# Two-layer cross-attention block, 128 sequences on one core: queries, keys and maxima turned on VectorE and moved by DMA in place of TensorE transposes

## The reference

```python
h = ln(x);  q, k, v = h@wq * 0.25, h@wk, h@wv;  q, k = rope(q), rope(k)
x = x + softmax(causal(q @ k.T)) @ v @ wo            # self-attention, "s"
h = ln(x);  q = rope(h@wq2 * 0.25);  k = rope(ctx@wk2);  v = ctx@wv2
x = x + softmax(q @ k.T) @ v @ wo2                   # cross-attention, "c"
x = x + gelu(ln(x)@fc1 + b1) @ fc2 + b2
a = softmax(x @ ctx.T) @ ctx
out = x + tanh(concat(x, a) @ trans_W + trans_b)
```

## Time and profile before

| | |
|---|---|
| median of 3 runs | 3412.29 us (3411.74 to 3413.0) |
| the profiled execution, its own time | 3413.38 us |
| its span in the profile | 3411.6 us |
| busy: PE, DVE, ACT, POOL | 3271.9, 2442.0, 2218.7, 1447.0 us |
| mean granted clock of TensorE | 0.983 of full speed |

### The profile page before, as it was taken

The page is one execution under the profiler, slowest core; times in us unless marked ns, Lnnn a source line. Parts: engine busy times, 40 slices in busy tenths (PEclk is TensorE's granted clock), DMA queues, the critical chain, the costliest instruction groups (busy, mean ns, idle before and its releaser), DMA issues.

```text
span 3411.6 us, 98793 instructions
## 1 busy us (share of the span) xinstructions
PE 3271.9 (96%) x40908; PEld 2779.5 (81%) x40908; DVE 2442.0 (72%) x5068; ACT 2218.7 (65%) x4737; POOL 1447.0 (42%) x2180
## 2 busy tenths in 40 slices
PE   3799999999999999999999999999999999999997
PEld 2588888888888888888888888888888888888886
DVE  3577777777777777777777777777777777777773
ACT  0366667667666666666676676666666666766764
POOL 0344444444444444444444444444444444444431
PEclk7799999999999999999999999999999999999998
DMA  3000000000000000000000000000000000000000
GB/s 88 20 16 20 27 20 20 27 20 20 27 20 22 25 20 27 21 20 27 20 20 27 20 20 27 20 22 25 20 26 21 20 27 20 20 27 20 20 13 10
DMA packets 83132, 79.62 MB, mean 23 GB/s; under 512 B 11904, under 2 KB 82432, under 8 KB 82688
## 3 DMA queue, kind: packets, MB, share of 16 engines
q1 hardware_dynamic: 82688, 73.30, 7.1%
HBM read 56.49 MB, written 16.78 MB: 21 GB/s over the span
## 4 chain that ended last, share of the span: by engine, by line
PE 87%; DVE 5%; POOL 4%; issue 3%; SPq 0%; ACT 0%; DMA 0%; DVEq 0%; POOLq 0%; ACTq 0%
PE sc L395 13%; PE A L365 12%; PE B L370 8%; PE B L372 6%; PE B L371 6%; PE B L443 4%; POOL kcf L1143 4%; PE C L370 3%; PE A L370 3%; PE C L372 3%; PE C L371 3%; PE A L371 3%; PE A L372 3%; PE A L454 3%; PE A L582 3%; PE B L365 3%
## 5 line engine op out<-in xcount | busy, mean ns | idle before, releaser
L1143 POOL TENSOR_TENSOR kcf<-tkc,rope_c 128x256 f32<-128x256 f32 x128 | 125.0, 976 | 687.7 <-DVE tkc L736 687.7
L749 DVE TENSOR_REDUCE qkz<-sc 128x8 f32<-128x1024 f32 x256 | 301.8, 1221 | 60.5 <-PE sc L385 60.5
L1007 ACT ACTIVATE pt_s<-sc 128x512 f32<-128x512 f32 x512 | 264.4, 604 | 114.1 <-PE sc L385 114.1
L749 DVE TENSOR_REDUCE qcz<-sc 128x8 f32<-128x1024 f32 x256 | 300.5, 1216 | 0.0
L1148 POOL TENSOR_TENSOR rstd<-bmv,eps_t 128x1 f32<-128x1 f32 x384 | 83.9, 219 | 441.4 <-DVE bmv L719 441.4
L1007 ACT ACTIVATE pt_c<-sc 128x512 f32<-128x512 f32 x512 | 264.6, 604 | 7.3 <-PE sc L395 5.9
L1143 POOL TENSOR_TENSOR qkf<-tqk,rope_c 128x512 f32<-128x512 f32 x128 | 210.8, 1647 | 121.4 <-DVE tqk L733 121.4
L365 PE MATMUL A<-ident,qkz 128*128 128x128 f32 x1536 | 240.5, 280 | 14.4 <-DVE qkz L793 8.2
L1150 POOL TENSOR_TENSOR rstd<-rstd,mhalf 128x1 f32<-128x1 f32 x384 | 234.8, 611 | 30.1
L973 ACT COPY kt_c<-A 128x512 f32<-128x512 f32 x128 | 75.1, 587 | 245.5 <-PE A L365 245.5
L1143 POOL TENSOR_TENSOR qcf<-tqc,rope_c 128x256 f32<-128x256 f32 x128 | 93.4, 729 | 326.0 <-DVE tqc L733 326.0
(11 more groups left out here) (230 smaller groups left out, 11606.1 us busy)
## 6 DMA issues: line engine op xcount, KB each, us to landing
rows_in<-in_x SPq DMA_DIRECT2D x128, 128.0 KB, 2.2
xt_f<-in_x_t SPq DMA_DIRECT2D x128, 128.0 KB, 2.2
rows_in<-in_ctx_t SPq DMA_DIRECT2D x128, 128.0 KB, 2.2
out<-o_out SPq DMA_DIRECT2D x128, 128.0 KB, 1.7
pt_s<-in_L_xattn_fc_w SPq DMA_DIRECT2D x1, 1024.0 KB, 5.0
rows_in<-in_L_xattn_fc_w SPq DMA_DIRECT2D x1, 1024.0 KB, 5.2
w_out_s<-in_L_xattn_sa_wo SPq DMA_DIRECT2D x4, 64.0 KB, 5.8
w_out_c<-in_L_xattn_ca_wo SPq DMA_DIRECT2D x4, 64.0 KB, 4.0
```

The source lines that it names most:

```text
L749: dve.tensor_reduce(out, sc[:, 2 * h:2 * h + 2, :].rearrange("p r (g k) -> p r g k", g=G), AX_X, ALU.max, negate=True).then_inc(signal, 1)
L1007: act.activation(pt[c][:, r, :, :].rearrange("p g q -> p (g q)"), sc[:, r, :], ACT.Exp).then_inc(signal, 1)
L1143: pool.tensor_tensor(out[:, :].rearrange("p (h e) -> p h e", e=HD), t[:, :].rearrange("p (h e) -> p h e", e=HD), rope_c[:, :].unsqueeze(1) ...
```

## The change

The six groups of four transposes per tile leave TensorE, and with them the two zero-padded layouts (`qkz`, `qcz`, `kcz`) and the six copies out of PSUM. In their place:

- `turn` (DVE) transposes 32x32 blocks of a 128x256 tile into `turned`: twice in `dtqk`, once each in `dtqc` and `dtkc`. `turn_maxima` (`dtms`, `dtmc`) does a 128x128 tile of maxima.
- `spread` (SP; steps `mvs` and `mvc`) issues 16 DMAs that put the pieces of queries and keys on their partitions; `move_maxima` (SP; `mvms` and `mvmc`) issues four that write the maxima. A tile now has 40 DMAs more: 44 instead of 4.
- The layout on the partitions is now `[row, group]`: a product reads every fourth element (`a[rows, :, g]`, 16 bytes apart) where it read neighbouring ones. `p2s` and `p2c` use 20 rows instead of 32.
- ACT rounds queries and keys from SBUF (`qt_s`, `kr_s`, `qt_c`, `kr_c`), four copies of 128x512 in place of six out of PSUM. The filler features are written once at the start, by three DMAs and five ACT copies.
- `addqk`, `addqc`, `addkc`, `rotqc`, `rotkc`, and the subtractions `xt_lo` and `ct_lo` go from DVE to GpSimd; `kr_s` and `kr_c` leave GpSimd.
- The steps get other lags, banks and orders on all five engines. `LAGS` goes from 8 to 11.

The core of the diff:

```diff
-LAGS = 8
+LAGS = 11
+            def spread(c, i, signal):
+                for b in range(G):
+                    for p in range(2):
+                        for h in range(2):
+                            rows, to = 32 * b + HD * h, 32 * (2 * p + h)
+                            sp.dma_start(qkt[c][i][to:to + HD, :, 32 * b:32 * b + 32, :].rearrange("e x q g -> e x (q g)"),
+                                         turned[c][rows:rows + HD, :, p, :, :].rearrange("e x t g -> e x (t g)")).then_inc(signal, 16)
+            def mvs(at):
+                    sp.wait_ge(s["dtqk"], 2 * n(at))
+                    need(sp, s["p2s"], n(at, -1))
+                    need(sp, s["qt_s"], n(at, -1))
+                    need(sp, s["kr_s"], n(at, -1))
+                    spread("s", at[1] % 2, mv["s"][at[1] % 4])
+            def mvc(at):
+                    sp.wait_ge(s["dtqc"], n(at))
+                    sp.wait_ge(s["dtkc"], n(at))
...
+            def move_maxima(c, i, signal):
+                for b in range(G):
+                    to = qt[c][i][MX:MX + 1, 32 * b:32 * b + 32, :]
+                    sp.dma_start(bass.AP(to.tensor, to.offset, [[32 * 2 * G * P, G], [1, 32 * G]]),
+                                 mxt[c][32 * b:32 * b + G, :, :].rearrange("r t g -> r (t g)")).then_inc(signal, 16)
...
+            def slot(i, u):                      # SP
+                mvms((i, u - 2))
+                io((i, u))
+                mvmc((i, u - 5))
+                mvc((i, u - 4))
+                mvs((i, u))
...
-                        mm = pe.matmul(sc[:, r, g * P:(g + 1) * P], a[rows, g, :], b[rows, g, :],
+                        mm = pe.matmul(sc[:, r, g * P:(g + 1) * P], a[rows, :, g], b[rows, :, g],
...
             def p2s(at):
-                    pe.wait_ge(s["qtm_s"], n(at))
-                    heads(kt["s"][at[1] % NB["kt_s"]], qtm["s"], 2 * HD, False)
+                    pe.wait_ge(s["mvms"], 64 * n(at))
+                    pe.wait_ge(mv["s"][at[1] % 4], moved(at))
+                    heads(kt["s"][at[1] % 2], qt["s"][at[1] % 2], MX + 1, False)
...
             def fy(at):
+                    pe.wait_ge(s["fatt_t"], n(at))
...
+            def turn(c, x, cols, signal):        # DVE
+                dve.transpose(turned[c][:, x, :, :, :].rearrange("q p t g -> q g p t"),
+                              cols.rearrange("q (g p j) -> q g p j", g=G, p=2)).then_inc(signal, 1)
+            def dtkc(at):
+                    dve.wait_ge(s["addkc"], n(at))
+                    need_moved(dve, "c", at)
+                    turn("c", 1, kcf[:, :], s["dtkc"])
...
+            def qt_c(at):                        # ACT
+                    act.wait_ge(mv["c"][at[1] % 4], moved(at))
+                    copy(qr["c"][:, :, :], qt["c"][at[1] % 2], s["qt_c"])
```

More of the change, by code:

```diff
@@ L42 @@
 RT = 2
-LAGS = 8
+LAGS = 11
 FIRST = 1
 AHEAD_X = 2
-AHEAD_C = 0
+AHEAD_C = -2
 AHEAD_T = 1
@@ L405, in vs @@
             def vs(at):
                 if live(at):
[L407 to L413, removed]
@@ L579, in fy0 @@
                 if live(at):
-                    after(at, (("fatt_t", 1, 1),))
+                    after(at, (("h3_lo", 1, 4),), (("ot_c", 1, 5),), (("tqc", 1, 7),), (("x3t", 1, 1),))
                     for k in range(KC):
-                        pe.matmul(A1[:, 0:E], x3t[at[1] % NB["x3t"]][:, k, :], w_t1[:, k, :], start=(k == 0),
+                        pe.matmul(A0[:, 0:E], x3t[at[1] % NB["x3t"]][:, k, :], w_t1[:, k, :], start=(k == 0),
                                   stop=False, skip_group_check=True)
@@ L586, in fy @@
                 if live(at):
-                    pe.matmul(A1[:, 0:E], fatt_t[:, :], cw[at[1] % NB["cw"]][:, :], start=False, stop=True,
+                    pe.wait_ge(s["fatt_t"], n(at))
+                    pe.matmul(A0[:, 0:E], fatt_t[:, :], cw[at[1] % NB["cw"]][:, :], start=False, stop=True,
                               skip_group_check=True).then_inc(s["fy"], 1)
@@ new lines, in slot @@
+                y_c((i, u - 6))
+                p1c((i, u - 5))
+                vcw((i, u - 5))
+                f1b((i, u - 7))
+                y_s((i, u - 3))
+                p2s((i, u - 2))
+                kvc((i, u - 4))
+                f2a((i, u - 7))
+                qk((i, u))
+                f2b((i, u - 7))
+                trx2((i, u - 3))
+                p2c((i, u - 5))
+                trf((i, u - 9))
+                pv_s((i, u - 2))
+                qc((i, u - 3))
+                fs((i, u - 9))
@@ L638, in _ @@
+                pv_c((i, u - 5))
+                vs((i, u))
+                trx3((i, u - 6))
+                p1s((i, u - 1))
+                trfa((i, u - 9))
+                fy0((i, u - 9))
+                fy((i, u - 9))
+                f1a((i, u - 6))
             steps(pe, slot)
@@ new lines, in slot @@
+            def slot(i, u):
+                norm_s((i, u - 3))
+                x2_((i, u - 6))
+                max_c((i, u - 5))
+                hla((i, u - 7))
+                dtmc((i, u - 5))
+                ln3((i, u - 6))
+                ln1((i, u))
+                dtqc((i, u - 4))
+                x1_((i, u - 3))
+                tkc_((i, u - 4))
+                hlb((i, u - 7))
+                tqk_((i, u))
+                dtkc((i, u - 4))
+                rotqk((i, u))
+                x3_((i, u - 7))
+                x2t_lo_((i, u - 3))
+                ln2((i, u - 3))
+                ot_s((i, u - 2))
+                tqc_((i, u - 3))
+                fmax_((i, u - 9))
+                dtqk((i, u))
+                ot_c((i, u - 5))
+                frec_((i, u - 9))
+                norm_c((i, u - 5))
+                h3_lo_((i, u - 6))
+                max_s((i, u - 1))
+                dtms((i, u - 1))
+                cw_((i, u - 5))
@@ L969, in _ @@
         def _(act):
+            act.wait_ge(ld_cst, N_CST)
+            for out, src in ((qt["s"][1], qt["s"][0]), (qt["c"][0], qt["s"][0]), (qt["c"][1], qt["s"][0]),
+                             (kt["s"][1], kt["s"][0]), (kt["c"][1], kt["c"][0])):
+                act.copy(out, src).then_inc(st_feat, 1)
             act.wait_ge(st_setup, 1)
@@ L1198, in xres_s_, with minus_hi @@
+            def minus_hi(out, a, hi, signal):
+                pool.tensor_tensor(out, a, hi.bitcast(F32), ALU.subtract).then_inc(signal, 1)
             def xres_s_(at):
@@ L1242, in shape_constants, with heads @@
     p = np.arange(P)
+    block, row = p // 32, p % 32 - HD
+    is_feature = (row >= 0) & (row < NF)
+    feat_q = is_feature[:, None] & (block[None, :] == row[:, None])
+    feat_k = is_feature[:, None] & (block[None, :] > row[:, None])
+    ones = (row == NF)[:, None] & (p >= 0)[None, :]
+    def heads(a):
+        return np.repeat(a.astype(f), G, 1)
     return {
+        "c_feat_q": heads(feat_q),
+        "c_feat_ks": heads(np.where(feat_k, AFTER, np.where(ones, 1.0, 0.0))),
+        "c_feat_kc": heads(ones),
         "c_ident": np.eye(P, dtype=f),
```

459 lines of the change are left out of this document (199 added, 260 removed).

## The result

The changed kernel takes 4742.09 us (median of 4 runs, 4737.86 to 4752.97) against 3412.01 us (4 runs): 1.3903 times the time of before, with a 95% interval of 1.3879 to 1.3927. The forecast was 3568 us and its range ended at 3800. The sign was right; the loss is 1330 us instead of 156.

What follows compares the result with a forecast made beforehand. TensorE's issue bounded the old kernel; a loop through SP's queue would bound the new: 6.24 + 1.3 + 17.3 + 1.8 = 26.6 us a slot. 3411.6 + 128 x (26.6 - 25.39) + 1.5 = 3568 us; range 3230 to 3800.

Steps and rivals of the forecast that it cites:

- The loop: From `p2s` through TensorE, DVE and SP's queue to the next slot's `p2s`: 26.6 us a slot against 25.39; chance 0.58.
- DVE's term: `tqk_` and `dtkc` on DVE with semaphores, between `qk` and `mvc`: 1.3 us of the slot.
- the landing: From the start of the last maximum's DMA issue to `p2s` of the next slot, with the signal: 1.8 us.
- POOL's additions: Additions moved to POOL: not in the loop; a wait on `kcf` in `dtkc` would mean up to 1 us more.
- the price of an issue: SP's queue: 0.494 us for each of 32 `spread` issues with the gap, 0.475 for others; 17.3 us in the loop.
- The rival of a queue that backs up: SP's issues cost 0.75 us, so the loop is 35.7 us and the time about 4730 us; chance 0.05.
- strides at "no change": Products reading elements 16 bytes apart keep their prices, 0.60 and 1.10 us; upper bound twice that.
- The third rival: Strided reads slow the products: `p2s` doubles, 1.1 us more in the loop, 27.7 us, about 3708 us; chance 0.12.
- TensorE's own sum: TensorE's work a slot if strided reads double the products: 25.4 us, still hidden behind the loop.
- the 0.15 for a first load: 0.15 us in the loop's TensorE part for the first weight load after a wait.
- Ends: Filling and draining the pipeline outside the full slots: about the same 160 us, give or take 40.

Runs made afterwards that it cites:

- the layout alone: Changed kernel with the DMAs of `spread` writing [group, row], so that nothing reads or writes with a stride: 4643.57 us.
- the sixteen matmuls alone: Changed kernel with sixteen matmuls that do nothing useful put on TensorE ahead of the wait of `p2s`: 4670.29 us.

## Why the prediction was right and wrong

**Right: the mechanism.** TensorE's six groups went, and what they gave went into waits before `p2s` (1.75 us in the slot shown, 393 us in all) and before `fy` (358 us), as said. The loop goes through `p2s`, `qk`, `tqk_`, `dtkc`, `mvc`, `mvs` and `mvms`, step for step. DVE's term (1.40 against 1.3) and the landing (1.60 against 1.8) held. POOL's additions aren't in the loop. Order and halving of the queue's work moved the time by hundreds of microseconds, as a loop through SP wants and a bound on TensorE or on the DMA engines doesn't.

**Wrong: the price of an issue, +6.2 us a slot.** The step was "I take the middle, 0.449, and with the gap 0.494 us". Every row behind it was of a transfer from DRAM. An issue from SBUF to SBUF takes 0.592 us, and two in a row start 0.635 apart. That makes 32 x 0.141 = 4.5 us. A long issue in this slot makes 1.2, for which the sum had no term, although had single issues of 988 and 1442 ns beside medians of 428 and 706. The maxima, 0.58 us apart, make 0.3, and the first two issues of `mvc` (0.67 and 0.64 us) with the gap ahead of `mvs` the last 0.2. The forecast had put an issue after idling at the cheap end. The range ended at 0.515; 0.635 lies inside the step's own bounds (0.415 to 0.75), but these had been narrowed. The rival of a queue that backs up gave 4730 us at 0.75 us an issue; that this is near the time measured is chance, since an issue took 0.635 and the DMA engines were 12% busy.

**Wrong: strides at "no change", +1.1 us in the loop.** The third rival had the right size: `p2s` went from 1.17 to 2.26 us. The stride of the stationary operand makes it. The Trainium skill, SBUF — State Buffer, section Door 1, has the rule on 16-byte lines that spoke against this layout, and for the weight load, ACT's copy and DVE's transposed output the traces agree (324 ns against 186, 1.1 us against 0.59, 0.66 against 0.42); for the moving operand of a product no run here shows a cost, and none reads it with the stride beside a stationary operand without one. The same rival's "TensorE's own sum would be 22.0 + 3.4 = 25.4" was near: with half of `spread`, TensorE is busy for 995.8 us in 1000 and the slot is 25.8 us. That is above the 25.39 of before, so even without the loop the layout alone takes the gain back.

**Missing: the clock, about +2.3 us.** The forecast put waits of 2 to 3 us before `p2s` and `fy` and kept the steps behind them at the prices of full clock. The trace shows them at 0.50: `kvc` 2.73 us against 1.51 and `f2a` 2.50 against 1.60, and the mask 0.2 longer. `p2s` with the stride takes 2.26 at either clock, as `p2c` at full clock shows; the 0.15 for a first load wasn't needed. The sum of the loop's excess is then 6.2 + 1.1 + 2.3, less 0.15, which is the 9.5 us of the table. These are prices in one slot. In the mean the slot is 8.8 us above the forecast, and since a shorter wait leaves less of the low clock, what a fix gives depends on what was fixed before it: the layout alone gave 0.7 us, the sixteen matmuls alone 0.7.

**Ends.** 4738.1 - 128 x 35.4 = 207 us for filling and draining against 160 give or take 40: just outside. That is 45 us of the 1174 by which the time missed; 128 x 8.8 = 1126 are the slot's.

The Trainium skill, DMA: Bandwidth & Descriptors, section Issuing engines are not separate DMA queues, says that the sequencer's time for starting a DMA is usually small beside the DMA itself. By this trace it isn't: 0.635 us of issue for a landing of 1.8.

**Open.** What the long issues are, and why an issue from SBUF to SBUF costs more. How much of the clock's 2.3 us a filled wait would give back alone. The moves of additions, rotations and subtractions to GpSimd were not tried by themselves.

## What to carry to other kernels

Price a DMA issue from a row with the same two memories, and follow every in-order queue as a loop: work on it before one semaphore, times its price, plus a landing. A stride of 16 bytes in a stationary operand doubles small products; let the DMA place the elements, which costs 8 ns an issue here. A wait of some microseconds on TensorE also takes away the clock of what stands behind it, so price those steps at both levels. Take the small part that pays alone: turned maxima, 8 KB a tile in four DMAs, gave 1.5%, and the whole change cost 39%.

## What the runs showed of the hardware that was not expected

- An issue on SP's queue: 0.423 us (median) from DRAM to SBUF, 0.439 from SBUF to DRAM (the store), 0.592 from SBUF to SBUF, the same for 8 and 16 KB, two or three dimensions, and 0.600 with eight runs on a partition. On ACT's queue 0.62, also with eight.
- A load of 20 to 32 rows x 128 float32 with a stride of 16 bytes: 324 ns against 186. ACT's copy of 128x512 writing so: 1.1 us against 0.59. DVE's block transpose of 128x256 writing so: 0.66 against 0.42.
- DVE's product of 128x512 in `rotqk` takes 1515 ns in the changed kernel and took 681 before. In the changed kernel GpSimd works on `tqk` at the same time, where before its product had ended 0.5 us ahead of `rotqk` in the slot looked at; that this is the cause wasn't tested. Its group after, in 1000 to 2000 us:

```profile
L764 DVE TENSOR_TENSOR rs_qk<-tqk,rope_s 128x512 f32<-128x512 f32 x28 | 42.4, 1515 | 0.0
```
